# A gated recurrence on one core: the last gate row repeated by TensorE, layer 0 of four tiles gathered on its own, and a new order of loads and rests

## What is computed

```
for i in range(6):
    gate = ih[i][token]                       # (2048, 256)
    state = tanh(state + matmul(state, hh[i]) * gate)
```

## Time and profile before

| | us |
|---|---|
| median of three runs | 105.87 |
| the profiled execution | 106.02 |
| its span | 104.2 |
| outside the span | 1.82 |
| TensorE busy | 87.1 (84%) |
| VectorE busy | 79.2 (76%) |
| ScalarE busy | 73.5 (70%) |
| GpSimd busy | 65.7 (63%) |

### The profile page before, as it was taken

One profiled execution on the slowest core, in us unless ns is written; L12 is line 12 of the kernel. 1 busy time (PEld: TensorE's weight loads), 2 busy tenths in 40 slices (PEclk: granted clock), 3 DMA queues, 4 the chain that ended last, 5 costly groups with the idle time before them and its releaser, 6 DMA issues.

```text
span 104.2 us, 1794 instructions
## 1 busy us (share of the span) xinstructions
PE 87.1 (84%) x650; PEld 74.4 (71%) x650; DVE 79.2 (76%) x127; ACT 73.5 (70%) x129; POOL 65.7 (63%) x60
## 2 busy tenths in 40 slices
PE   5919909895498998987999989999899998999900
PEld 5817608474386896976898978999789897898800
DVE  2179085283979399996979879798897978989990
ACT  4078020891897818799799996999969999667431
POOL 2687787734043008694897939979398893992440
PEclk9995885589999999999999999999999999999998
DMA  3899999999699915542387523555319654095355
GB/s 39 285 367 401 417 388 376 315 307 347 205 215 268 188 36 101 104 79 48 75 58 145 97 60 58 101 101 101 72 29 86 121 101 94 18 130 221 147 201 201
DMA packets 27128, 17.46 MB, mean 168 GB/s; under 512 B 22421, under 2 KB 22677, under 8 KB 27120
## 3 DMA queue, kind: packets, MB, share of 16 engines
q1 hardware_dynamic: 24816, 13.64, 55.2%
q0 software_dynamic: 2304, 3.71, 9.9%
HBM read 19.14 MB, written 2.10 MB: 204 GB/s over the span
## 4 chain that ended last, share of the span: by engine, by line
PE 51%; DMA 16%; DVE 13%; issue 9%; SPq 3%; ACT 3%; POOL 2%; POOLq 0%; DVEq 0%
PE products L278 38%; PE turned L310 7%; DMA state<-in_state_rows 6%; DVE sums L434 5%; DMA gates<-in_gate_rows,index 5%; PE products L270 5%; DMA w_full<-in_weights 5%; DVE sums L442 4%; ACT gates L336 1%; POOL sums L262 1%; DVE split_rows L455 1%; DVE split_cols L448 1%; ACT state L372 1%; SPq L190 1%; POOL gates L255 1%
## 5 line engine op out<-in xcount | busy, mean ns | idle before, releaser
L262 POOL TENSOR_TENSOR sums<-sums,state 128x512 f32<-128x512 f32 x37 | 46.8, 1274 | 21.4 <-DVE sums L434 20.5
L278 PE MATMUL products<-w_head,split_cols 128*128 128x256 f16 x316 | 54.8, 273 | 1.5 <-issue 1.5
L372 ACT ACTIVATE state<-sums 128x512 f32<-128x512 f32 (+1 forms) x49 | 30.2, 619 | 19.9 <-DVE sums L442 10.9
L278 PE MATMUL products<-w_rest,split_cols 128*128 128x256 f16 x158 | 43.1, 273 | 0.0
L278 PEld LDWEIGHTS products<-w_head,split_cols 128*128 128x128 f16 x316 | 30.9, 98 | 5.8 <-issue 2.3
L434 DVE SCALAR_TENSOR_TENSOR sums<-products,w_down,gates 128x512 f32<-128x512 f32 (+1 forms) x40 | 29.3, 735 | 0.3 <-PE products L278 0.2
L270 PE MATMUL products<-w_full,first_cols 128*128 128x256 f32 x64 | 20.1, 471 | 8.7 <-DMA first_cols<-in_state_cols 6.0
L270 PEld LDWEIGHTS products<-w_full,first_cols 128*128 128x128 f32 x64 | 14.5, 237 | 13.6 <-DMA first_cols<-in_state_cols 7.4
L255 POOL DMA_INDIRECT gates<-in_gate_rows,index x13 | 14.3, 1099 | 10.2 <-ACT gates L336 6.8
L278 PEld LDWEIGHTS products<-w_rest,split_cols 128*128 128x128 f16 x158 | 15.4, 98 | 1.7
L455 DVE SCALAR_TENSOR_TENSOR split_rows<-copies,split_rows 128x512 f16<-128x512 f32 x19 | 13.0, 686 | 3.9 <-ACT split_rows L360 3.7
(11 more groups left out here) (30 smaller groups left out, 28.5 us busy)
## 6 DMA issues: line engine op xcount, KB each, us to landing
first_cols<-in_state_cols SPq DMA_DIRECT2D x8, 256.0 KB, 5.0
state<-in_state_rows SPq DMA_DIRECT2D x8, 256.0 KB, 5.9
out<-state SPq DMA_DIRECT2D x7, 256.0 KB, 2.0
w_full<-in_weights SPq DMA_DIRECT2D x6, 256.0 KB, 5.2
last_row<-in_gate_rows SPq DMA_DIRECT2D x1, 768.0 KB, 4.6
split_cols<-split_rows SPq DMA_TRANSPOSE x19, 3.1
gates<-in_gate_rows,index POOLq DMA_INDIRECT x16, 5.5
out<-state SPq DMA_DIRECT2D x2, 128.0 KB, 1.9
```

The lines of the kernel that those rows point to most:

```text
L262: nc.gpsimd.tensor_tensor(sums[:, q], sums[:, q], pair_rows(state, q), ALU.add).then_inc(pool_added, 1)
L278: last = nc.tensor.matmul(bank[:, j, :], split_cols[:, q, s, j, k, :], w[:, l - 1, k * HID:(k + 1) * HID], start=(n == 0), stop=(n == len( ...
L372: nc.scalar.activation(pair_rows(state, q)[:, cut], sums[:, q, cut], ACT.Tanh).then_inc(state_ready, 1)
```

## The change

It does seven things.

1. The last row is loaded once, 6 KB onto one partition (into the part of `sums` that is not in use yet). TensorE multiplies it with a row of ones, three matmuls of 512 columns in fp32 into three PSUM banks, and VectorE copies the banks into `last_rows`. Fills wait for the three copies. `WARM` goes from 9 to 3.
2. Tiles 0 to 3 get layer 0 alone, by four full gathers of 1 KB per row, ahead of all others. Layers 1 to 5 of these tiles are filled and gathered with bounds like the others, after tiles 4 to 15. So no gather of 768 KB is left, and there are 20 gathers where there were 16.
3. ScalarE fills seven tiles ahead of step 0 (three before) and tiles 0 and 1 after steps 1 and 2. VectorE fills three ahead of step 0 (five before), then 9, 11 and, after step 3, 2 and 3. The fills of tiles 0 to 3 are five layers long.
4. SyncE loads by pairs: turned state, state, and weights with some. From pair 2 on each pair waits until the state of two pairs before has landed, and no longer for products. `LOAD_LAG` is 8, so transposes come behind all loads in its program.
5. `REST_LAG` goes from 4 to 5 and `REST_ROWS_LAG` from 2 to 3.
6. The side work on the weights moves: totals after products 4 and 8 (3 and 9 before), VectorE's scales after steps 2 and 8, heads after steps 3, 9, 17, 25, 33 (3, 12, 20, 28, 36), rests after 5, 11, 19, 27, 35 (4, 13, 21, 29, 37).
7. In layer 5 VectorE adds the state for pairs 2, 6 and 7 (3, 5 and 7 before). The pairs that TensorE turns are the same (`PE_INSTEAD` names the one that `LAST_TURN` named).

```diff
-    LAST_TURN = (LAST - 1, PAIRS - 1)
+    PE_INSTEAD = ((4, 7),)
-    REST_LAG, REST_ROWS_LAG = 4, 2
-    LAST_ON_DVE = (3, 5, 7)
-    WHOLE = 3
-    ACT_FILLS = {-1: (4, 7, 10), 1: (12,), 3: (14,)}
-    DVE_FILLS = {-1: (3, 5, 6, 8, 9), 0: (11,), 2: (13,), 3: (15,)}
+    REST_LAG, REST_ROWS_LAG = 5, 3
+    LAST_ON_DVE = (2, 6, 7)
+    FIRST = (0, 1, 2, 3)
+    GATHERS = (4, 5, 6, 7, 8, 9, 10, 11, 12, 13, 14, 15, 0, 1, 2, 3)
+    ACT_FILLS = {-1: (5, 8, 10, 12, 13, 14, 15), 1: (0,), 2: (1,)}
+    DVE_FILLS = {-1: (4, 6, 7), 0: (9,), 1: (11,), 3: (2, 3)}
-    SUMS_AT = {0: 0, 2: 1, 3: 2, 4: 3, 5: 4}
-    TOTALS_AT = {3: 0, 9: 1}
-    HEADS_AT = {3: 0, 12: 1, 20: 2, 28: 3, 36: 4}
-    RESTS_AT = {4: 0, 13: 1, 21: 2, 29: 3, 37: 4}
-    WARM = 9
+    SUMS_AT = {0: 0, 2: 1, 3: 2, 4: 3, 6: 4}
+    TOTALS_AT = {4: 0, 8: 1}
+    SCALES_AT = {2: 0, 8: 1}
+    HEADS_AT = {3: 0, 9: 1, 17: 2, 25: 3, 33: 4}
+    RESTS_AT = {5: 0, 11: 1, 19: 2, 27: 3, 35: 4}
+    WARM = 3
-    LOAD_LAG = 3
+    LOAD_LAG = 8
+    AHEAD = 2
+    WEIGHTS_WITH = {0: (0, 1), 1: (2,), 2: (3,), 3: (4,), 7: (5,)}
+    ROW_BANKS = 3
...
+        last_row = sums[0:1, PAIRS - ROW_BANKS:].rearrange("p q j h -> p (q j h)")
+        row_banks = [turned[0]..., turned[1]..., copies[0]...]
...
+            def load_pair(q):
+                if q >= AHEAD:
+                    sp.wait_ge(rows_in[q - AHEAD], 16)
+                load_cols(q)
+                if q == 0:
+                    load_weights(0)
+                load_rows(q)
+                for l in WEIGHTS_WITH.get(q, ()):
+                    if l > 0:
+                        load_weights(l)
+            sp.dma_start(last_row[:, :], gate_rows[VOCAB - 1:VOCAB]).then_inc(last_in, 16)
...
+            for t in FIRST:
+                pool.indirect_dma_start(gates[:, t, 0, :], None, gate_first, offset(t)).then_inc(first_in[t // PAIR], 16)
+            for t in GATHERS:
...
+            pe.wait_ge(last_in, 16)
+            for n in range(ROW_BANKS):
+                nc.tensor.matmul(row_banks[n], ones[0:1, :], last_row[:, n * PAIR * HID:(n + 1) * PAIR * HID],
+                                 start=True, stop=True).then_inc(row_repeated, 1)
...
+            for n in range(ROW_BANKS):
+                dve.wait_ge(row_repeated, n + 1)
+                nc.vector.tensor_copy(last_rows[:, n * PAIR * HID:(n + 1) * PAIR * HID],
+                                      row_banks[n]).then_inc(last_rows_ready, 1)
...
                 if layer == 0:
+                    dve.wait_ge(first_in[q] if PAIR * q in FIRST else gates_in[q], 16 * PAIR)
+                elif layer == 1 and PAIR * q in FIRST:
                     dve.wait_ge(gates_in[q], 16 * PAIR)
```

More of the change, by code:

```diff
@@ L3, with gated_recurrence @@
 from contextlib import ExitStack
-def gated_recurrence(nc, token, state_cols, state_rows, weights, gate_rows, out):
+def gated_recurrence(nc, token, state_cols, state_rows, weights, gate_first, gate_later, gate_rows, out):
     fp32, fp16 = mybir.dt.float32, mybir.dt.float16
@@ L63, in gated_recurrence @@
     INDEX_STEPS, SCALE_STEPS = 3, 4
-    LOAD_LAG = 3
+    LOAD_LAG = 8
+    AHEAD = 2
+    WEIGHTS_WITH = {0: (0, 1), 1: (2,), 2: (3,), 3: (4,), 7: (5,)}
+    ROW_BANKS = 3
     PRODUCTS, TURNED, COPIES = 3, 2, 2
     def by_dma(i):
-        return order[i][0] < LAST and order[i][1] in DMA_PAIRS and order[i] != LAST_TURN
+        return order[i][0] < LAST and order[i][1] in DMA_PAIRS and order[i] not in PE_INSTEAD
     def by_pe(i):
@@ L75, in on_pool @@
         layer, q = order[i]
-        return layer > 0 and not (layer == LAST and q in LAST_ON_DVE)
+        return layer > 0 and not (layer == LAST and q in LAST_ON_DVE) and order[i] not in MORE_ON_DVE
     def pe_turns(i):
@@ L91, in landed @@
     def landed(l, q):
-        return 16 * (l + 1)
+        return 16 * sum(by_dma(at[n, q]) for n in range(l + 1))
     def cuts(i):
@@ L138, in gated_recurrence @@
         spare = ps("spare", [P, PAIR, HID], fp32)
+        row_banks = [turned[0][:, :, :, :].rearrange("p j k r -> p (j k r)"),
+                     turned[1][:, :, :, :].rearrange("p j k r -> p (j k r)"),
+                     copies[0][:, :, :].rearrange("p j h -> p (j h)")]
         tok_in = sem("tok_in")
@@ L244, in _, with offset @@
             by_vector = [t for tiles in DVE_FILLS.values() for t in tiles]
[L245 to L250, removed]
+            def offset(t):
+                return bass.IndirectOffsetOnAxis(ap=index[:, t:t + 1], axis=0)
+            for t in FIRST:
+                pool.indirect_dma_start(gates[:, t, 0, :], None, gate_first, offset(t)).then_inc(first_in[t // PAIR], 16)
+            for t in GATHERS:
                 if t in by_act:
@@ L292, in product @@
                     pe.wait_ge(rest_ready, pe_turns(at[layer - 1, q]))
-                if layer > 0 and q == 0:
+                if layer > 0 and i == min(at[layer, p] for p in range(PAIRS)):
                     pe.wait_ge(w_rest_ready, layer)
@@ L334, in fill @@
             def fill(t):
-                act.wait_ge(last_in, 16)
-                nc.scalar.activation(gates[:, t].rearrange("p l h -> p (l h)"), last_row[:, :],
+                act.wait_ge(last_rows_ready, ROW_BANKS)
+                lo = 1 if t in FIRST else 0
+                nc.scalar.activation(gates[:, t, lo:, :].rearrange("p l h -> p (l h)"), last_rows[:, lo * HID:],
                                      ACT.Copy).then_inc(act_filled, 1)
```

49 lines of the change are left out of this document (23 added, 26 removed).

## The result

The changed kernel took 99.35 us in the median of four runs (98.58, 99.05 and 99.66; a fourth execution took 486.92 us; without it the median is 99.05). The kernel before took 106.66 in the median of four beside it. The ratio is 0.934, with a 95% interval from 0.928 to 0.940. The profiled execution took 99.66 us, its span is 97.9, and 1.76 lies outside. The forecast was 101.0, from 98.0 to 104.3, and the forecast case itself 99.3 to 102.8.

What follows compares the result with a forecast made beforehand. Layer 0 was taken as bound by transfers and the low clock in their waits, later time by TensorE's matmul count. 35.0 to G plus 63.8 gave 98.8, plus 1.82 outside 100.6, stated as 101.0; range 98.0 to 104.3.

Steps and rivals of the forecast that it cites:

- Last row: Start of the kernel: row landed at 3.0, matmuls 5.1 us to 8.1, all rows ready at 8.9, 3.1 us later than before.
- Fills and first tanh: ScalarE in layer 0: seven fills of 1.37 us put the first tanh at 18.6 instead of 14.47.
- Product 4 at the lower clock: TensorE in layer 0: after waiting for the first tanh, product 4 takes 3.4 us against 1.7.
- G: Start of step 8's gate product, first of layer 1: 38.54 before, predicted 35.0, or 33.3 at full clock.
- Gathers: GpSimd's queue of 20: sixteenth bounded gather leaves at 29.4, lands at 34.6 to 35.0, so G is no less than 33.7.
- From G to the end: Layer 1 to the end: 65.7 us becomes 63.8, 1.5 off at starts of layers 3 to 5, 0.4 in the tail.
- one more step of lag costs and brings nothing: Rest lags after G: one more step costs VectorE nothing, the same instructions in another order.
- Load pacing: Loads in layer 0: 5.5 MB done by about 21; what the lighter start frees is hidden by fills up to step 3.
- Earlier still: Rival in layer 0: clock rises within the repeats and stays up, first tanh at 17, G worth 32.1, 98.0 us; chance 0.14.
- Late gathers: Rival in layer 0: last gather lands at 37.6 to 38, G worth 36.7, 102.5 to 104 us; chance 0.10.
- The transposes kept their cover: Rival at layer crossings: transposes lose cover, level with before from about 5.6 us landings, 109 us at 6.2; chance 0.07.
- the change does nothing but save the 1.9 us behind: Rival: fills and low clock replace transfers in layer 0, G stays 38.5, only 1.9 us after it won, 104.1 us; chance 0.12.

Runs made afterwards that it cites:

- Four fills first: Changed kernel with four instead of seven ScalarE fills ahead of the first tanh, tiles 12 to 15 and 0 filled behind later steps: 99.92 us, ratio 0.943.
- last row by DMA: Changed kernel with the last row loaded onto all partitions by one 768 KB DMA and nine warm matmuls: 99.01, 103.08, 103.15 and 104.88 us.
- weights late: Changed kernel with heads and rests of the weights of layers 2 to 5 at the old, later steps: 100.54 us, ratio 0.950.
- tile 0 whole: Changed kernel with layers 1 to 5 of tile 0 gathered in full behind the four first gathers, without its fill: 100.93 us, ratio 0.952.
- adds on 3, 5 and 7: Changed kernel with VectorE's adds of layer 5 on pairs 3, 5 and 7 again: 100.47 us, ratio 0.948.
- no later gathers: Changed kernel without the gathers of layers 1 to 5 of tiles 0 to 3, so part of the computation is missing: 98.99 us, ratio 0.935.
- gathers as before: Changed kernel with tiles 0 to 2 gathered whole and the old tables of fills, last row still by TensorE: 103.04 us, ratio 0.966.

## Why the prediction was right, step by step

**Last row.** Right in sum: the repeats began at 2.67 for 3.0, took 5.5 us for 5.1, at the lower clock, and ended at 8.16 for 8.1; third copy done at 8.89 for 8.9. A matmul with one row costs what a full one does, as the row of 1x512 shows.

**Fills and first tanh.** 18.55 for 18.6. Four fills first showed that it is these fills that bound the tanh, and that their length is not what layer 0 costs in the end.

**Product 4 at the lower clock.** Wrong: 1.89 us for 3.4. My reason was that TensorE would be idle from 16 on, after the 2.89 us of the earlier trace rows. But products 0 and 1 ran at the lower clock, up to 13.85, so the four ended at 18.09, and the wait was 1.13. Nor would the longer wait have been enough: without the later gathers it was 2.59 us, and product 4 took 1.89 all the same. VectorE's idle time ahead of the first scales was 1.95 instead of 4. Step 8 came at 33.16; the prediction had 35.0, and 33.3 for full clock. This is G as the prediction defines it: 1.8 us early, with 64.7 us behind it instead of 63.8.

**Gathers.** The queue was underpriced. The last gather was issued at 32.61, not 29.4: the first bounded one began at 10.70, not 9.9, and six issues ahead of the last took longer than 0.99 us, 2.5 us in all (1.80 and 1.51 the longest). The trace before had such issues, 1.79, 1.44, 1.31 and 1.40 us at 5.97, 8.07, 9.81 and 14.02, all beside fills of VectorE; the prediction took 0.99 for each. The last gather landed in 3.9 us, where I had taken 5.2 to 5.6, so at 36.5 instead of 34.6 to 35.0. Step 9 waited 0.90 us for it; the run without these gathers moved step 9 by 0.6 and the time by nothing that can be told. The Trainium skill (DMA: Bandwidth & Descriptors, Anatomy of one DMA — SWDGE (gpsimd) path) gives by its fit an estimate of 2.2 us for such a gather; the shortest bounded one of the changed kernel took 3.0.

These two errors have opposite signs, and that they cancel is luck. By step 9's gate product at 36.61, less the 1.26 us between steps 8 and 9 before, G is worth 36.61 - 1.26 = 35.35, against 35.0. The value was right, the reason was not: step 9 is held by the gather queue, and 0.9 us behind it by VectorE's scales of total 1, which now stand between steps 8 and 9. The prediction's 1.3 us from G to step 9 had no room for them.

**From G to the end.** Counted from that value, 97.9 - 35.35 = 62.5 us for 63.8, so 3.2 us won where I had 1.9. The tail gave 0.6 (5.44 us from the last matmul's start to the end before, 4.82 after), I had 0.4. The stalls at layer starts gave 2.4: not only the three of 0.29 us with their refill, but also the one of 0.63 at layer 2, which I had left as it was. Total 1's wait of 1.5 us was as predicted. The forecast of 101.0 is 1.65 us over the median: 0.9 of it lies in the span (98.8 for 97.9), 0.4 was an allowance for stalls in layer 1 that no row had.

**The step that failed: one more step of lag costs and brings nothing.** On the kernel before it brings nothing that the times can tell. In the changed kernel it is worth 4.8 us, 2.6 at step 9 and about 2.3 behind. I had counted instructions, which are the same, and asked only whether the transposes keep their cover. The waits of VectorE for ScalarE's heads of rows stood in the trace before, 3.2 us from 50 us on, and I had not read that row. The other half, a transpose that meets the last gather, stood in the earlier trace rows as the longest landing: the transpose of 5.2 us was issued at 32.30, with the gather of 31.24, which took 5.4, in flight. I had read it as a bound for the transposes alone.

**Load pacing.** I had put it under the fills, worth nothing. By the timeline that holds, no product waits for a load. But it is a condition: with the old order, pacing and place of the transposes together, the changed kernel loses 8.5 us. An edit that hides is not an edit that can be left out.

**Rivals.** "Earlier still" (98.0) was nearer in time than the forecast: the clock did stay up, but the rise came after the repeats, at 13.85, and the gathers gave back what it won. Late gathers happened in part: the last landed at 36.5, between the forecast's 35.0 and that rival's 37.6. The transposes kept their cover: their landings are 3.0/3.1/4.0 and no product waited for one. That the change does nothing but save the 1.9 us behind is refuted by step 9, 3.2 us earlier.

**What stays open.** The single undoings from step 9 on (2.3 for the lags, 1.0 weights, 1 total, 0.8 tail) sum to 5 us, and 3.1 were won, so they share slack; how much each gives in every combination was not run. Why transposes and gathers cost each other 2 to 5 us in some traces and little over 1 in others is not shown by any run, nor whether layer 0 without such a meeting would gain from an earlier first tanh.

## What to carry to other kernels

Price the edits of one change together: a lag, a pacing or an order can be worth next to nothing alone and five us in company, so read every row of waits of the engine that it touches, also those that bound nothing yet. Before an engine's start is moved ahead, ask which transfers move with it and what they meet. An idle stretch of one engine is free only as long as the one behind it is the later one, as total 1 showed.

## What the runs showed of the hardware

- **A DMA transpose and a gather of GpSimd's queue, in flight together, can take far longer.** A transpose of this size took 3.1 us in the median, and without any gather up to 5.0 (kernel before, at 51.69). Together with gathers the three of the changed kernel took 3.3 to 4.0 us, the gathers 3.0 to 4.3. In two traces they took much more: transposes 5.7 and 8.1, gathers 6.1 and 7.1 (a length that gathers reach, at 6.1, under the loads of layer 0 too). While a transpose's packets run, those of the gathers nearly stop: in the us from 32 of the changed kernel 10 of them start beside 640 of the transpose, and with the last row by DMA 43 and 20. The DMA engines then show a share of 0.93 to 1.22 at 115 to 169 GB/s.
- **A matmul of one row costs a full one.** Six instructions for three fp32 matmuls of 512 columns, 0.85 us apart at half clock, where the products' matmuls of 256 columns and 128 rows are 0.43 apart. The Trainium skill (TensorE: Matmul & The Clock Gate, Step-by-step: what each phase is for) says that loading weights scales with columns and that rows don't matter; the trace agrees for the pair of load and matmul.
- **VectorE and GpSimd slow each other.** Four of the long gather issues (1.16 to 1.80 us instead of 0.99) overlap fp32 copies of VectorE, as four did in the kernel before; the other two long ones (1.49) begin within 0.1 us of an add of VectorE. The rests of the weights took nearly twice as long beside GpSimd's adds (min/median/max in ns of L445):

```profile
L445 DVE SCALAR_TENSOR_TENSOR w_rest<-w_full,w_up,w_head x5: 748/1379/1387, 28.9 to 76.7; 128x512 f16<-128x512 f32 x5
```

  The Trainium skill (GPSIMD Engine Reference, Specifications) says that GpSimd's SBUF interfaces are shared with VectorE, with contention for VectorE's instructions with two SBUF inputs or in a 2-port mode. The traces agree: this instruction reads two tensors in SBUF. The four beside an add took 1.23 to 1.39 us, the fifth 0.75; in the kernel before and in the run with the weights late none was beside an add, and all ten took 0.75. From 50 us on it cost nothing, since TensorE has no idle time there.
- **The length of one wait does not say whether the clock falls.** It stayed full through waits of TensorE of 1.1 to 1.6 us, and also of 2.33 (tile 0 whole), 2.47 (adds on 3, 5 and 7) and 2.59 us (no later gathers). It went to half after 1.89 us (four fills first) and 2.06 us (gathers as before), and after or during waits of 2.60, 4.13 and 4.79 us, for 3.4, 10.2 and 6.8 us.
